# Giving GpSimd every fourth chunk of the weighting in the attention's second pass

## The chip, the cores and the metric

The kernel runs on one core of a Trainium2 chip. The metric is the device time of one execution in microseconds (us), median of several runs. The engines are named as in the profile: PE (TensorE), DVE (VectorE), ACT (ScalarE), POOL (GpSimd) and SP (SyncE, which only issues DMAs here).

## The reference

Four graph layers follow one another, each added to the node features and layer-normed. The change is in the third, graph attention: 3125 nodes of 256 features (8 heads of 32), 100000 edges sorted by destination.

```python
h = (x @ W.T).reshape(n, H, D)
h_src = h[src]
...
alpha = jnp.where(alpha >= 0, alpha, 0.2 * alpha)
amax = jax.ops.segment_max(alpha, dst, num_segments=n)
ex = jnp.exp(alpha - amax[dst])
denom = jax.ops.segment_sum(ex, dst, num_segments=n)
attn = ex / jnp.maximum(denom[dst], 1e-10)
out = jax.ops.segment_sum(h_src * attn[..., None], dst, num_segments=n)
return out.reshape(n, H * D) + bias
```

## The kernel before

The edges are padded and cut into `NCD` = 808 chunks of 128 edges, so that one chunk belongs to one block of 128 destination nodes; there are `NB` = 25 blocks. The attention has two passes over the chunks. The first (`logits_*`) gathers the source rows, writes them to `rows_spill` in HBM and keeps logits and running maxima in SBUF. The second (`sums_*`, with `carry_vector` ahead of it) makes the weighted sums. Since `denom` is the same for all edges of a node, it sums the unnormalised messages and the weights together, `TW` = 264 columns, and divides at the end (`attention_end_vector`).

For chunk c of the second pass:

- SP loads the 128 x 256 spilled rows into `hs`, a ring of `RB` = 16 slots in the tile `big`; slot c may be refilled when the rows of chunk c - 16 are weighted (L1972).
- ACT makes the one-hot matrices of four chunks at a time (`oh3`, L1996 and L1998), and the exponentials of four chunks at a time (L2005), written into columns 256 to 263 of the message buffers `msg`, a ring of 8 in the tile `ring`. The exponentials of group i (chunks 4i to 4i+3) wait until PE has summed chunk 4i - 5, since the buffers of group i - 2 must be free.
- `weighted_rows` (L1979) multiplies the 256 row entries by the weight of their head and writes `msg[:, c % 8, 0:256]`. It waits for the exponentials of its group, for the rows, and for PE having summed chunk c - 8. Both inputs, `hs` and the broadcast weights in `msg`, lie in SBUF.
- PE multiplies the one-hot matrix by the message into PSUM bank c % 8 (L2032, two MATMUL records for each chunk), in the order of the chunks.
- DVE adds the bank to the block's slice of the accumulator `hsrc`, in the tile `big` (L2069). The slice is picked by a number from a register; L83 loads sixteen such numbers at a time, L84 moves one. Two chunks in turn mostly add to the same slice, and so each add waits for the end of the add before:

```python
v.wait_ge(summed.s, summed.n(c + 1))
if c >= 1:
    v.wait_ge(added.s, added.n(c))
here = big[:, bass.ds(blk.at(c) * TW, TW)]
```

DVE's order is written out by hand in `sums_vector`: the weighting of chunk n, then the add of chunk n - 4, and so on. POOL has two instructions at the start of the pass, the cast L1984 of `off_last` into `away_b` and the memset L1985 of the accumulator, and then waits at the barrier `meet()` until the pass is over. Every engine's waits are on semaphores; `n(k)` is the count that k events give.

Of the kernel before, what the change touches and what calls it, by code (L numbers as in the profile page):

```python
# [9 lines left out]
def up(n, m):  # L10
    return -(-n // m) * m
# [17 lines left out]
NCD = up((E + (P - 1) * NB) // P, 8)  # L29
# [57 lines left out]
def program(nc, t, out):  # L87
    with ExitStack() as ctx:
        v, a, pe, g, sp = nc.vector, nc.scalar, nc.tensor, nc.gpsimd, nc.sync
        known = {}  # L90

        def signal(name):
            if name not in known:
                known[name] = Signal(ctx.enter_context(nc.semaphore(name)))
            return known[name]

        def again(old, count):

            new = Signal(old.s)
            new.over(old.base + count)  # L100
            return new
# [52 lines left out]
        def lanes(col, n, k):  # L154
            return col.rearrange("p (n o) -> p n o", o=1).to_broadcast([col.shape[0], n, k])
# [1589 lines left out]
        RB = 16  # L1745
# [219 lines left out]
        aways_made = again(mids_g, 0)  # L1965
        exps, msgs_v = again(step_done, NBATCH + 1), again(prefix_kept, NBATCH)

        def sums_sync():
            for c in range(NCD):
                if c >= RB:  # L1970
                    sp.wait_ge(msgs_v.s, msgs_v.n(c - RB + 1))
                sp.dma_start(hs[:, c % RB, :], rows_spill[c]).then_inc(spill.s(c, RB), 16)  # L1972

        def weighted_rows(eng, c):
            eng.wait_ge(exps.s, exps.n(c // 4 + 1))
            eng.wait_ge(spill.s(c, RB), spill.n(c, RB))
            if c >= 8:
                eng.wait_ge(summed.s, summed.n(c - 7))
            return eng.tensor_tensor(msg[:, c % 8, 0:D].rearrange("p (h d) -> p h d", h=H),  # L1979
                                     hs[:, c % RB, :].rearrange("p (h d) -> p h d", h=H),  # L1980
                                     lanes(msg[:, c % 8, D:TW], H, HD), ALU.mult)

        def sums_pool():
            g.tensor_copy(away_b[:, 1, :], off_last).then_inc(aways_made.s, 1)  # L1984
            g.memset(hsrc, 0.0).then_inc(accs_zeroed.s, 1)  # L1985

        def sums_scalar():
            a.copy(ident_b3, ident)
            a.copy(away_b[:, 0, :], off_first).then_inc(aways_made.s, 1)
            for n in range(NCD + 6):  # L1990
                if n < NCD and n % 4 == 0:
                    i, hot = n // 4, oh3[n // 4 % OH3]
                    if i >= OH3:
                        a.wait_ge(summed.s, summed.n(4 * (i - OH3) + 4))
                    for k in range(4):
                        ins = a.activation(hot[:, k, :], iota, ACT.Abs, bias=recd3[:, n + k, D_DL:D_DL + 1], scale=-1.0)  # L1996
                    then_a(ins)
                    a.activation(hot, hot, ACT.Relu, bias=1.0, scale=-1.0).then_inc(hot_made.s, 1)  # L1998
                c = n - 6
                if c >= 0 and c % 4 == 3:  # L2000
                    i = c // 4
                    a.wait_ge(lowered.s, lowered.n(1 if 4 * i + 4 <= CH else 2))
                    if i >= 2:
                        a.wait_ge(summed.s, summed.n(4 * i - 4))
                    a.activation(msg[:, 4 * (i % 2):4 * (i % 2) + 4, D:TW], alpha[:, 4 * i:4 * i + 4, :],  # L2005
                                 ACT.Exp).then_inc(exps.s, 1)

        def away_tensor(k):

            cs = slice(k // (2 * H) * CH, (k // (2 * H) + 1) * CH)  # L2010
            pe.matmul(ps[k % 8][:, 0:CH], ident_b3, away_b[:, k % 2, cs], start=True, stop=False)

        def sums_tensor():
            pe.wait_ge(aways_made.s, aways_made.n(2))
            for k in range(8):
                away_tensor(k)
            pe.wait_ge(carried.s, carried.n(1))
            for k in range(4 * H):
                half, h, reach = k // (2 * H), k // 2 % H, (fwd, bwd)[k % 2]
                if k >= 8:  # L2020
                    pe.wait_ge(carry_used.s, carry_used.n(k - 7))
                    away_tensor(k)
                pe.matmul(ps[k % 8][:, 0:CH], lanes(ident[0:H, h:h + 1], 1, P)[:, 0, :],
                          reach[:, half * CH:(half + 1) * CH], start=False, stop=True).then_inc(carry_spread.s, 1)
            pe.wait_ge(carry_used.s, carry_used.n(4 * H))
            pe.wait_ge(accs_zeroed.s, accs_zeroed.n(1))
            for c in range(NCD):
                pe.wait_ge(hot_made.s, hot_made.n(c // 4 + 1))
                pe.wait_ge(msgs_v.s, msgs_v.n(c + 1))
                if c >= 8:  # L2030
                    pe.wait_ge(added.s, added.n(c - 7))
                pe.matmul(ps[c % 8][:, 0:TW], oh3[c // 4 % OH3][:, c % 4, :], msg[:, c % 8, :],  # L2032
                          start=True, stop=True).then_inc(summed.s, 1)
# [22 lines left out]
        def sums_vector():  # L2056
            blk = Numbers(v, regs_v, blk_d_row, NB - 1)
            v.wait_ge(accs_zeroed.s, accs_zeroed.n(1))
            for n in range(NCD + 4):
                c = n  # L2060
                if c < NCD:
                    weighted_rows(v, c).then_inc(msgs_v.s, 1)
                c = n - 4
                if c >= 0:
# [4 lines that stand above are left out]
                    v.tensor_tensor(here, here, ps[c % 8][:, 0:TW], ALU.add).then_inc(added.s, 1)  # L2069
            v.wait_ge(added.s, added.n(NCD))  # L2070

        sums_sync()
        sums_pool()
        sums_scalar()
        sums_tensor()
        carry_vector()
        sums_vector()
        summed.over(NCD)
        added.over(NCD)
# [137 lines left out]
```

## Time and profile before

| | |
|---|---|
| median of 3 runs | 8846.99 us (8846.64 to 8849.97) |
| profiled execution, its own time | 8844.68 us |
| its span, first to last instruction | 8842.9 us |
| second pass's loop over the chunks, from the first weighting (L1979) | from 7024.5 us on; last L1979 starts at 7630.6 us |
| instructions of L1979, L2069 | 808 each, all on DVE |

The profile is of one execution. Busy time is the time in which an engine worked on instructions; an instruction's record covers its whole duration, and on DVE the next one can start before the record of the last has ended, so the distance from start to start says what an instruction costs a busy engine. Idle time is put down to what ended last before the engine went on.

### The profile page before, as it was taken

The page shows a single profiled execution, that of the slowest core. Times are in us where ns is not written, and L with a number is a line of the kernel's source. Part 1 is how long each engine was busy: PE and PEld are TensorE (multiplying, and loading weights), DVE is VectorE, ACT ScalarE, POOL GpSimd, SP SyncE. Part 2 cuts the span into 40 slices and gives each one's busy share as a digit, 9 for nine tenths or more (in the row PEclk, how much of TensorE's full clock was granted, in tenths as well). Part 3 has the DMA queues.
Part 4 walks back from the last instruction along what each step waited for, and adds up shares of the span by engine and source line. Part 5 has one row for each costly group of instructions (what it writes and reads, how often), then busy time and mean ns, then how long its engine had stood idle before and what let it go on. Part 6 is the DMA issues. An engine that isn't in the chain of part 4 may idle for free. (4 is left out here: it accounts for less than half of the span.)

```text
span 8842.9 us, 98679 instructions
## 1 busy us (share of the span) xinstructions
PE 5516.0 (62%) x21277; PEld 3079.4 (35%) x21277; DVE 5795.6 (66%) x15735; ACT 2945.2 (33%) x9436; POOL 5601.3 (63%) x5671
## 2 busy tenths in 40 slices
PE   2224980000677777777767777756767789687775
PEld 1113770000444444444532222343333333333332
DVE  8999980000777775555559999877777799833333
ACT  0000220000566652222238888733333366300000
POOL 5777777776777766777537777527777300077775
PEclk9999775555788888888869999977666699866665
DMA  2001320001555554555548888628888555333334
GB/s 94 6 6 40 117 86 11 3 3 38 158 166 159 160 143 148 166 161 166 151 120 242 242 242 242 175 80 243 244 243 243 136 175 176 102 105 105 105 105 87
DMA packets 796177, 1192.24 MB, mean 135 GB/s; under 512 B 161213, under 2 KB 631923, under 8 KB 788941
## 3 DMA queue, kind: packets, MB, share of 16 engines
q0 software_dynamic: 259712, 606.96, 26.1%
q1 hardware_dynamic: 535885, 578.95, 20.5%
q8 instruction: 192, 3.15, 0.1%
q14 instruction: 388, 3.18, 0.1%
HBM read 926.73 MB, written 258.64 MB: 134 GB/s over the span
## 5 line engine op out<-in xcount | busy, mean ns | idle before, releaser
L1178 POOL DMA_INDIRECT ring<-scaled_table,idx_s x832 | 787.3, 946 | 1024.9 <-DVEq L193 771.8
L1405 POOL DMA_INDIRECT big<-y_table,idx_s x832 | 859.5, 1033 | 480.3 <-issue 246.3
L1794 POOL DMA_INDIRECT ring<-att_table,rec_d_sb x808 | 778.9, 964 | 458.6 <-DVEq L193 206.4
L1473 PE MATMUL bank<-big,wts 128*128 128x512 f32 x1664 | 831.9, 623 | 364.0 <-DVE big L1397 364.0
L334 POOL DMA_INDIRECT rec_s<-acc,big x784 | 836.4, 1067 | 322.4 <-issue 256.5
L1034 POOL DMA_INDIRECT big<-x_table,rec_d_sb x808 | 812.2, 1005 | 300.5 <-issue 227.3
L2147 PE MATMUL bank<-ring,acc 128*128 128x256 f32 x1664 | 829.8, 621 | 239.3 <-DMA ring<-scaled_table,idx_s 202.3
L1178 POOL DMA_INDIRECT ring<-h_table,rec_d_sb x808 | 765.0, 947 | 310.7 <-issue 201.7
L334 POOL DMA_INDIRECT rec_d<-x_res,big x784 | 750.6, 957 | 255.7 <-issue 255.7
L1813 PE MATMUL bank<-big 128*128 x2424 | 594.4, 373 | 273.0 <-DVE acc L1904 219.0
L1215 PE MATMUL bank<-ring,acc 128*128 128x256 f32 x1616 | 549.0, 466 | 225.4 <-DMA ring<-h_table,rec_d_sb 222.6
L1421 ACT ACTIVATE big<-big,ring 128x64 f32<-128x64 f32 x2496 | 673.6, 332 | 19.3 <-DMA big<-y_table,idx_s 19.3
L1200 DVE TENSOR_TENSOR acc<-acc,bank 128x256 f32 x808 | 340.4, 421 | 461.2 <-PE bank L1215 239.9
L2137 DVE TENSOR_TENSOR acc<-acc,bank 128x256 f32 x416 | 175.3, 421 | 705.2 <-PEq L2150 630.4
L2147 PEld LDWEIGHTS bank<-ring,acc 128*128 128x128 f32 x1664 | 380.4, 277 | 688.5 <-DMA ring<-scaled_table,idx_s 637.6
L1473 PEld LDWEIGHTS bank<-big,wts 128*128 128x128 f32 x1664 | 284.8, 191 | 910.5 <-DVE big L1397 657.1
L2032 PE MATMUL bank<-ring 128*128 128x264 f32 x1616 | 545.8, 424 | 65.9 <-issue 58.8
L1139 PE MATMUL bank<-big,acc 128*128 128x256 f32 x1616 | 500.1, 454 | 116.4 <-DVE acc L1094 101.5
L1040 DVE MEMSET acc<- 128x512 f32 x1 | 0.5, 485 | 851.7 <-POOLq L193 851.7
L974 PE MATMUL bank<-ident,rec_d_sb 128*128 128x128 f32 x28 | 5.2, 373 | 868.8 <-DMA rec_d_sb<-rec_d 868.8
L1855 ACT ACTIVATE wts<-bank 128x256 f32<-128x256 f32 x808 | 310.2, 384 | 672.8 <-PE bank L1818 616.8
L833 ACT ACTIVATE big<-bank,big 128x128 f32<-128x128 f32 x832 | 312.6, 376 | 476.9 <-PE bank L801 474.5
(348 smaller groups left out, 12643.2 us busy)
## 6 DMA issues: line engine op xcount, KB each, us to landing
weights_dram<-big SPq DMA_DIRECT2D x104, 1024.0 KB
big<-weights_dram SPq DMA_DIRECT2D x832, 128.0 KB, 3.5
rows_spill<-ring SPq DMA_DIRECT2D x808, 128.0 KB
big<-rows_spill SPq DMA_DIRECT2D x808, 128.0 KB, 2.2
ring<-key_dram SPq DMA_DIRECT2D x49, 1024.0 KB
big<-dl_dram SPq DMA_DIRECT2D x50, 512.0 KB
big<-y_table,idx_s POOLq DMA_INDIRECT x832, 4.0
ring<-scaled_table,idx_s POOLq DMA_INDIRECT x832, 2.8
```

The lines of the kernel that those rows point to most:

```text
L334: g.indirect_dma_start(out=table, out_offset=bass.IndirectOffsetOnAxis(ap=row_of[k][:, j:j + 1], axis=0), in_=stage[:, j, :], in_offset=No ...
L1034: g.indirect_dma_start(out=xg[:, c % RG, :], out_offset=None, in_=x_table, in_offset=bass.IndirectOffsetOnAxis(ap=recd3i[:, c, D_IDX:D_IDX ...
L1139: ins = pe.matmul(quarter_bank(c), onehot[:, c % 16, :], xg[:, c % RG, 0:D], start=True, stop=True)
L1178: g.indirect_dma_start(out=slot[:, c % ring_len, :], out_offset=None, in_=table, in_offset=bass.IndirectOffsetOnAxis(ap=index(c), axis=0)) ...
L1215: ins = pe.matmul(quarter_bank(c), hot20[:, c % 20, :], hg[:, c % R2, :], start=True, stop=True)
L1405: g.indirect_dma_start(out=yg[:, n % RY, :], out_offset=None, in_=y_table, in_offset=bass.IndirectOffsetOnAxis(ap=idx_s[:, n:n + 1], axis= ...
L1421: ins = a.mul(dots[:, c % (2 * RM), d * MUL:(d + 1) * MUL], vectors[:, d * MUL:(d + 1) * MUL], sh3[:, c, d:d + 1])
L1473: pe.matmul(ps[4 + u % 4], oh1[c // 4 % 2][:, c % 4, :], mid[:, c % (2 * RM), 0:512], start=(c % 2 == 0), stop=(c % 2 == 1)).then_inc(summ ...
L1794: g.indirect_dma_start(out=ag[:, n % R3, :], out_offset=None, in_=att_table, in_offset=bass.IndirectOffsetOnAxis(ap=recd3i[:, n, D_IDX:D_I ...
L1813: ins = pe.matmul(ps[c % 3][:, 0:TW], hot_n[:, i % 3, k * P:(k + 1) * P], big_b[:, bass.ds(at + s * TW, TW)], start=(s == 0), stop=(s == 2))
L2032: pe.matmul(ps[c % 8][:, 0:TW], oh3[c // 4 % OH3][:, c % 4, :], msg[:, c % 8, :], start=True, stop=True).then_inc(summed.s, 1)
L2147: pe.matmul(ps[u % 8][:, 0:D], oh20[:, c % 20, :], sg[:, c % R4, :], start=(c % 2 == 0), stop=(c % 2 == 1))
```

## The change

In `weighted_rows` nothing changes. Chunks 3, 7, 11, ... are now weighted on POOL, which counts them on a new semaphore `msgs_by_pool`; DVE leaves them out and counts its own 606 on the old one. Whoever waits for a weighted chunk (PE before its matmul, SP before it refills a slot of `hs`) asks `rows_done`, which picks the semaphore by the chunk's number. The order of the adds on DVE, ACT's work and all buffers stay.

```diff
+        msgs_g = signal("msgs_by_pool")
+
+        def rows_done(eng, c):
+            if c % 4 == 3:
+                eng.wait_ge(msgs_g.s, msgs_g.n(c // 4 + 1))
+            else:
+                eng.wait_ge(msgs_v.s, msgs_v.n(c + 1 - (c + 1) // 4))
+
         def sums_sync():
             for c in range(NCD):
                 if c >= RB:
-                    sp.wait_ge(msgs_v.s, msgs_v.n(c - RB + 1))
+                    rows_done(sp, c - RB)
...
             g.memset(hsrc, 0.0).then_inc(accs_zeroed.s, 1)
+            for c in range(3, NCD, 4):
+                weighted_rows(g, c).then_inc(msgs_g.s, 1)
...
-                pe.wait_ge(msgs_v.s, msgs_v.n(c + 1))
+                rows_done(pe, c)
...
-                if c < NCD:
+                if c < NCD and c % 4 != 3:
                     weighted_rows(v, c).then_inc(msgs_v.s, 1)
```

The first place is DVE's queue in the middle of the pass, before. L1979 is a weighting, L84 the register move, L2069 an add:

```order
L84 ISA
L2069 TENSOR_TENSOR big<-big,bank 128x264
L1979 TENSOR_TENSOR ring<-big,ring 128x256
L84 ISA
L2069 TENSOR_TENSOR big<-big,bank 128x264
L1979 TENSOR_TENSOR ring<-big,ring 128x256
L84 ISA
L2069 TENSOR_TENSOR big<-big,bank 128x264
L1979 TENSOR_TENSOR ring<-big,ring 128x256
```

The same place now, where the weighting has line L1987 and the add L2079:

```order
L2079 TENSOR_TENSOR big<-big,bank 128x264
L1987 TENSOR_TENSOR ring<-big,ring 128x256
L84 ISA
L2079 TENSOR_TENSOR big<-big,bank 128x264
L84 ISA
L2079 TENSOR_TENSOR big<-big,bank 128x264
L1987 TENSOR_TENSOR ring<-big,ring 128x256
L84 ISA
L2079 TENSOR_TENSOR big<-big,bank 128x264
```

Once in four chunks two adds now stand next to each other, with no weighting between them.

The second place is POOL's queue, now, from the end of the first pass (L1794 is its gather) into the second; `blocks_counted` is the semaphore that counts the exponentials:

```order
L1794 DMA ring<-att_table,rec_d_sb 128x264 [waits mids_v,spill3]
L1992 CAST big<-rec_d_sb 128x808 [waits engines_met]
L1993 MEMSET big 128x6600
L1987 TENSOR_TENSOR ring<-big,ring 128x256 [waits spill3,blocks_counted]
L1987 TENSOR_TENSOR ring<-big,ring 128x256 [waits spill7,blocks_counted]
L1987 TENSOR_TENSOR ring<-big,ring 128x256 [waits summed,spill11,blocks_counted]
```

The three weightings shown are the first of 202; before, the memset was followed by the gathers of the fourth layer.

The third is PE's queue, now, in the middle of the pass (`prefix_kept` is the old count of weighted chunks):

```order
L2042 MATMUL bank<-ring 128x264 [waits added,msgs_by_pool,hot_made]
L2042 MATMUL bank<-ring 128x264 [waits added,prefix_kept,hot_made] x3
L2042 MATMUL bank<-ring 128x264 [waits added,msgs_by_pool,hot_made]
L2042 MATMUL bank<-ring 128x264 [waits added,prefix_kept,hot_made] x3
```

Before, all of them waited for `prefix_kept`; the order of the matmuls is the same.

## Rows read from the trace of the kernel before

**Rows 1.** The page: busy time of each engine.
```profile
span 8842.9 us, 98679 instructions
PE 5516.0 (62%) x21277; PEld 3079.4 (35%) x21277; DVE 5795.6 (66%) x15735; ACT 2945.2 (33%) x9436; POOL 5601.3 (63%) x5671
```

**Rows 2.** Engines by stretch: stretch, its length, busy (instructions), granted clock, DMA share, GB/s.
```profile
core 0: us, PE busy (x) PEld busy (x) DVE busy (x) ACT busy (x) POOL busy (x), PEclk, DMA share, GB/s
...
7024.50:7631.00 606.50, 544.99 (x1614) 241.50 (x1614) 550.49 (x1613) 400.32 (x1185) 0.00 (x0) 1.00 0.59 172
```

**Rows 3.** The instructions of L1979: count, shortest, median and longest duration.
```profile
L1979 DVE TENSOR_TENSOR ring<-big,ring x808: 408/418/426, 7024.5 to 7630.6; 128x256 f32<-128x256 f32 x162
```

**Rows 4.** Instructions in order of time, the middle of the pass: start, duration, engine, line.
```profile
7299.24 0.42 DVE L1979 TENSOR_TENSOR ring<-big,ring 128x256 f32<-128x256 f32 x1
...
7299.58 0.42 DVE L2069 TENSOR_TENSOR big<-big,bank 128x264 f32 x1
...
7299.92 0.42 DVE L1979 TENSOR_TENSOR ring<-big,ring 128x256 f32<-128x256 f32 x1
7300.25 0.42 DVE L2069 TENSOR_TENSOR big<-big,bank 128x264 f32 x1
7300.41 0.30 PEld L2032 LDWEIGHTS bank<-ring 128*128 128x128 f32 x2 [0.38 <-issue]
7300.54 0.23 ACT L2005 ACTIVATE ring<-acc 128x32 f32<-128x32 f32 x1 [0.64 <-PE bank L2032]
```

**Rows 5.** Instructions in order of time, DVE at the end of the pass.
```profile
7630.63 0.42 DVE L1979 TENSOR_TENSOR ring<-big,ring 128x256 f32<-128x256 f32 x1
7630.97 0.42 DVE L2069 TENSOR_TENSOR big<-big,bank 128x264 f32 x1
7631.61 0.43 DVE L2069 TENSOR_TENSOR big<-big,bank 128x264 f32 x1 [0.22 <-DVE big L2069]
7632.26 0.43 DVE L2069 TENSOR_TENSOR big<-big,bank 128x264 f32 x1 [0.22 <-DVE big L2069]
7632.91 0.43 DVE L2069 TENSOR_TENSOR big<-big,bank 128x264 f32 x1 [0.22 <-DVE big L2069]
```

**Rows 6.** The register loads L83 of the pass.
```profile
L83 DVEq TENSOR_LOAD <-unit_numbers x51: 1095/1099/1120, 7026.4 to 7627.7; - x51
```

**Rows 7.** Instructions in order of time, the pass's start, where PE had messages waiting.
```profile
7027.87 3.31 PE L2032 MATMUL bank<-ring 128*128 128x264 f32 x12
```

**Rows 8.** Instructions in order of time, POOL and DVE at the start of the second pass.
```profile
6950.56 1.83 DVE L2037 TENSOR_TENSOR_SCAN big<-rec_d_sb,norm 8x808 f32<-8x808 f32 x1 [1.29 <-ACTq L193]
6950.59 3.23 POOL L1984 CAST big<-rec_d_sb 128x808 bf16<-128x808 f32 x1 [16.43 <-ACTq L193]
...
6952.31 3.20 DVE L2038 TENSOR_TENSOR_SCAN big<-rec_d_sb,small 8x808 f32<-8x808 f32 x1
...
6953.77 5.59 POOL L1985 MEMSET big<- 128x6600 f32 x1
```

**Rows 9.** Groups by line and shape in the first pass: forward and reversed scans.
```profile
L1931 DVE TENSOR_TENSOR_SCAN ring<-ring 128x128 f32<-128x128 f32 x50 | 21.5, 429 | 4.5
L1926 DVE TENSOR_TENSOR_SCAN ring<-ring,bank 128x128 f32<-128x128 f32 x50 | 21.0, 420 | 3.7 <-issue 0.2
```

**Rows 10.** POOL's smallest memset, in the groups by line and shape.
```profile
L2207 POOL MEMSET const-float32-1.0<- 128x1 f32 x1 | 0.1, 104 | 0.0
```

**Rows 11.** The waits in the pass: who waited for whom, total, times, longest.
```profile
PE bank L2032 <- issue: 58.8, 60, 1.5
DVE big L2069 <- PE bank L2032: 55.3, 62, 1.4
PEld bank L2032 <- ACT ring L1998: 23.3, 59, 0.7
```

## The prediction

> **What bounds the kernel now.** I read the busy times first [rows 1]: no engine is near the whole span, so each stage has to be read by itself. The stage of the change is the loop over 808 chunks, and the view by stretches shows it [rows 2]: 606.5 us, with DVE busy for 550 us and PE for 545 us at a granted clock of 1.00 (the upper level, 2.4 GHz), POOL not at all, and the DMA engines 59% busy. Two engines near 90% can mean either, so I went to the order of time.
>
> There [rows 4] DVE alternates without a gap: a weighting at 7299.24, an add at 7299.58, a weighting at 7299.92, an add at 7300.25. From start to start it is 0.34 us each, 0.675 us for a chunk, and 807 x 0.675 = 545 us. The loop takes 606.1 us from the first to the last weighting [rows 3]; most of the other 61 us are the 51 register loads of 1.10 us each, 56 us [rows 6], which show as 62 adds that waited [rows 11]. PE is not the bound: each chunk's weights are loaded 0.07 us after its weighting ended (7299.92 + 0.42, against 7300.41 in [rows 4]), so PE takes each message as it comes; where messages were waiting for it, 12 matmul records, six chunks, took 3.31 us, 0.55 us a chunk [rows 7]. The pass runs at DVE's pace.
>
> Then the question is what DVE's 0.675 us consist of. The end of the pass answers it, where adds follow each other with no weighting between [rows 5]: they start at 7630.97, 7631.61, 7632.26 and 7632.91, 0.65 us apart, with 0.22 us idle each, released by the add before. An add waits for the end of the add before it (0.42 us), and semaphore, register move and start take the other 0.23 us. So the chain of adds alone needs 0.65 us a chunk, and the weighting lies almost wholly inside that wait.
>
> **The change, part by part.**
>
> *What is taken from DVE.* 202 weightings of 0.34 us of DVE's time, 68 us in a simple count. By the chain of adds, four chunks cost 3 x 0.675 + 0.65 = 2.675 us where they cost 2.70: the gain is 0.025 us in four chunks, 202 x 0.025 = 5 us. The 51 register loads stay as they are.
>
> *What POOL does.* 202 multiplications of two SBUF operands, 128 x 256, f32. No row has one, so I bound it. The memset of 6600 elements took 5.59 us [rows 8], 0.1 us of it fixed [rows 10], so a write costs 0.83 ns an element; at that rate 256 take 0.32 us, the lower bound. The cast of 808 elements is recorded with 3.23 us, but see below: it worked for 1.43 us, which is 1.65 ns an element beside the fixed part, so a read costs about 0.8 ns. Two reads and a write are then 2.45 ns, and 256 of them 0.63 us, 0.73 with the fixed part. I take 0.70 us. For the upper bound I take the cast's recorded 4.0 ns an element: 1.03 us. At 0.7 us in every 2.7 POOL has time enough, and PE gets POOL's chunk early: it may be made as soon as chunk c - 8 is summed, seven chunks ahead.
>
> The Trainium skill ("GPSIMD Engine Reference", section "Performance versus the Vector engine") gives 4497 ns for a two-input f32 operation of 2048 elements, about 2.6 cycles an element; as an estimate from that page 256 elements take 0.56 to 0.62 us. The sum below would by that be 12 to 21 us smaller. No row here shows it.
>
> *What it does to DVE.* The start of the pass has the one place where POOL and DVE both read SBUF in this kernel [rows 8]. DVE's scan L2037, with two SBUF inputs, starts at 6950.56 and takes 1.83 us; POOL's cast starts 0.03 us later and ends only at 6953.82. DVE's second scan L2038, of the same shape, starts at 6952.31 and takes 3.20 us, 1.37 more. That it runs backwards doesn't explain it: in the first pass forward and reversed scans take 420 and 429 ns [rows 9]. It fits one after the other: scan to 6952.39, cast to 6953.82 (1.43 us), second scan from there 1.69 us to 6955.51. So POOL's read and DVE's two-input instruction exclude each other for their whole length, on two instances. The memset that follows reads nothing.
>
> The Trainium skill ("SBUF — State Buffer", "Who interferes with whom") says the same as a rule: a DVE instruction with two SBUF inputs contends with a GpSimd instruction that reads SBUF, and the second to come blocks until the first is finished. It speaks against this change: the weightings have two SBUF inputs on both engines. The add has one of its two inputs in PSUM, and by that page doesn't contend; no row here shows an add beside a reading POOL.
>
> *Where in the period it hits.* Count from the start of DVE's weighting of chunk 4j+2 (0). The adds follow at 0.34 and 0.99, the weighting of 4j+4 at 1.33, an add at 1.66, weighting 4j+5 at 2.00, an add at 2.34, weighting 4j+6 at 2.675. POOL's next operation waits for exponentials that wait for PE having summed 4j+3. A weighting's start to the exponential that waits for its matmul is 1.30 us (7299.24 to 7300.54 in [rows 4]); the second matmul adds 0.55 [rows 7], the exponential 0.23, a semaphore 0.07: POOL may start at 2.15. DVE is then in weighting 4j+5 until 2.34. POOL runs from 2.34 to 3.04, under the add, and weighting 4j+6, due at 2.675, waits 0.36 us. Behind it in DVE's queue stands the add, so the whole chain of adds is late, and PE, which waits for that message, with it.
>
> In one period of four the register load (it stands behind the weighting of chunk 16k+4) holds DVE from about 1.66 to 2.77; POOL runs in that hole, from 2.15 to 2.85, and is done before the weighting behind it. That leaves 202 - 51 = 151 stalls: 151 x 0.36 = 54 us.
>
> *What else is added.* PE's and SP's waits only change their semaphore. POOL's queue has nothing behind the weightings but the barrier; the gathers of the fourth layer come after it. ACT waits in each group for PE now (0.64 us in [rows 4]) and keeps that slack. The rows' DMAs, 59% busy, are asked for a little more slowly. All this I cost at nothing. PE lies open wherever DVE stalls.
>
> *Sum.* -5 + 54 = +49 us. The profiled execution took 8844.68 us, 2.3 below the median of 8847; on the median the forecast is 8896 us, slower by 0.55%. By the bounds of POOL's operation: at 1.03 us the stall is 0.69, the sum +99 (8946 us); at 0.32 us it ends with the add and nothing stalls, -5 (8842 us).
>
> **The rivals.** A measurement of this kernel can tell about 0.2%, 18 us, from no change.
>
> *Contention as above* (forecast), 72% with POOL's operation between about 0.48 and 1.03 us. Another 7% I give to an operation longer than that, as with a slow broadcast operand: at 1.5 us each period loses about 1.1 us, the hole of the register load covers less, and it comes to over 200 us.
>
> *No exclusion between multiplications.* The scans may be special, and two instances are few. Then POOL's work is hidden, the chain of adds decides, and the time is 8842 us. 9%.
>
> *POOL asks later.* If POOL starts 0.5 us later than I reckon, after weighting 4j+6 has begun, it runs from 3.01 to 3.71, under the two adds that stand together; the next weighting is due at 4.0. No stall: 8842 us again. It decides at 2.675 against my 2.15. 8%.
>
> *DVE's instructions are the bound, not the chain* (the other side). If the second of the two adds needn't wait for the first, each period saves the whole 0.34 us: 68 us, less some stalls, 8779 to 8830 us. The 0.22 us of idle time at the end of the pass [rows 5] speaks against it; 4%.
>
> **How the numbers follow.** Slower by over 0.2% is 72 + 7, less 1 for stalls that come to under 18 us: 0.78. Within 0.2%: 9 + 8 and that 1: 0.18. Faster: 0.04. The range reaches from the cases without stalls, 8842, with a few us below, to the upper bound of POOL's operation, 8946, and a little over for the handing over at each conflict: 8838 to 8955 us. Outside lie the long operation and the faster case, about 11%, and a few per cent at the edges.
>
> **What would show it.** After the change the loop takes some 655 us from the first to the last weighting. POOL shows 202 multiplications, about 0.7 us by start and end, many starting while a weighting of DVE runs. DVE's 606 weightings are no longer all 0.42 us long: about a quarter of them (one in four chunks, save those at register loads) last about 0.36 us longer, or start that late. Some 200 adds have 0.22 us idle ahead of them, released by an add. If the weightings all keep 0.42 us and the loop is 600 us, the exclusion is wrong; if the adds stand closer than 0.65 us, the chain is wrong; if POOL's operation has another length, the stall changes by as much. The prediction fails most easily by POOL's length, and by where in the period POOL asks.

## The result and the profile after

The changed kernel takes 8875.1 us (median), the kernel before beside it 8848.9 us: a ratio of 1.0029, interval 1.0023 to 1.0035, 26 us slower. The profiled execution of after took 8879.5 us, its span is 8877.7 us, 34.8 more than that of before; of these two executions the parts are compared below. In the experiments' first two sets (e1 to e8) the kernel before took 10028 and 10040 us, in the third (e9 to e12) 8838 us; the added time lies in the stages with indirect DMAs, while the second pass's loop of an unchanged DVE queue takes 606 us in all of them (e1, e2, e8, e12), so e1 to e8 are read by this loop and by single instructions, and only e9 to e12 by totals too.

First the weightings of the pass and the adds, after (duration shortest, median, longest; first and last start):

```profile
L1987 DVE TENSOR_TENSOR ring<-big,ring x606: 411/420/833, 7052.7 to 7664.2; 128x256 f32<-128x256 f32 x152
L1987 POOL TENSOR_TENSOR ring<-big,ring x202: 614/840/844, 7019.7 to 7659.7; 128x256 f32<-128x256 f32 x101
```

```profile
  PE bank L2042: 54.6, 59
  DVE big L2079: 44.8, 203
  issue: 0.5, 2
```

The second fence is what the adds of L2079 waited for. Two things are to be seen. From DVE's first weighting to its last the loop takes 7664.2 - 7052.7 = 611.5 us, where it took 606.1 [rows 3]: 5.4 us more. And it begins 28 us later than before, 7052.7 against 7024.5. So in these two executions 28 of the 35 us were lost before the loop had begun, in stages whose code is the same.

The groups of the pass by line, where the mean of DVE's weighting has gone from 418 to 439 ns:

```profile
L2079 DVE TENSOR_TENSOR big<-big,bank 128x264 f32 x808 | 342.3, 424 | 99.9 <-PE bank L2042 54.6 <-DVE big L2079 44.8 <-issue 0.5
L1987 DVE TENSOR_TENSOR ring<-big,ring 128x256 f32<-128x256 f32 x606 | 265.9, 439 | 0.5
...
L1987 POOL TENSOR_TENSOR ring<-big,ring 128x256 f32<-128x256 f32 x202 | 156.3, 774 | 516.7 <-ACT ring L2015 516.7
```

One period of four chunks in order of time, the counterpart of [rows 4] (L2015 makes the exponentials, L2042 is the matmul):

```profile
7303.95 0.43 DVE L2079 TENSOR_TENSOR big<-big,bank 128x264 f32 x1 [0.22 <-DVE big L2079]
7304.29 0.42 DVE L1987 TENSOR_TENSOR ring<-big,ring 128x256 f32<-128x256 f32 x1
7304.63 0.42 DVE L2079 TENSOR_TENSOR big<-big,bank 128x264 f32 x1
7304.71 0.23 ACT L2015 ACTIVATE ring<-acc 128x32 f32<-128x32 f32 x1 [0.94 <-PE bank L2042]
...
7304.97 0.42 DVE L1987 TENSOR_TENSOR ring<-big,ring 128x256 f32<-128x256 f32 x1
7305.02 0.84 POOL L1987 TENSOR_TENSOR ring<-big,ring 128x256 f32<-128x256 f32 x1 [2.16 <-ACT ring L2015]
7305.30 0.42 DVE L2079 TENSOR_TENSOR big<-big,bank 128x264 f32 x1
...
7305.64 0.50 DVE L1987 TENSOR_TENSOR ring<-big,ring 128x256 f32<-128x256 f32 x1
```

POOL starts 0.05 us into a weighting of DVE and takes 0.84 us. The add between isn't touched. The next weighting, at 7305.64, takes 0.50 us in place of 0.42: it is held for 0.08 us.

Of the 606 weightings 137 are held, 131 of them for 0.08 us like this one. The other six are held for 0.13 to 0.41 us. In the longest case POOL had begun 0.06 us before DVE, and it kept its short duration:

```profile
7132.17 0.61 POOL L1987 TENSOR_TENSOR ring<-big,ring 128x256 f32<-128x256 f32 x1 [3.18 <-ACT ring L2015]
7132.23 0.83 DVE L1987 TENSOR_TENSOR ring<-big,ring 128x256 f32<-128x256 f32 x1
```

All 137 follow one rule to within 0.01 us: the weighting is held for what was left of POOL's record when it started, less 0.14 us (here 7132.78 - 7132.23 - 0.14 = 0.41). The seven weightings that started in the last 0.10 us of a record of POOL weren't held.

Ahead of the pass the difference is in POOL's indirect DMAs. The scatters L334 at the program's start, the gathers L1405 of a middle stage, the gathers L1794 of the first attention pass and L1178 of the last stage, before:

```profile
L334 POOL DMA_INDIRECT rec_s<-acc,big x784: 954/958/2535, 53.2 to 1161.2; - x196
L334 POOL DMA_INDIRECT rec_d<-x_res,big x784: 952/958/971, 1162.4 to 2167.5; - x196
...
L1405 POOL DMA_INDIRECT big<-y_table,idx_s x832: 942/949/1269, 4537.4 to 5695.4; - x167
...
L1794 POOL DMA_INDIRECT ring<-att_table,rec_d_sb x808: 942/946/2312, 5903.0 to 6933.2; - x162
...
L1178 POOL DMA_INDIRECT ring<-scaled_table,idx_s x832: 942/946/1032, 7731.1 to 8770.6; - x167
```

and after:

```profile
L334 POOL DMA_INDIRECT rec_s<-acc,big x784: 962/967/2599, 53.2 to 1164.7; - x196
L334 POOL DMA_INDIRECT rec_d<-x_res,big x784: 962/967/979, 1166.0 to 2177.5; - x196
...
L1405 POOL DMA_INDIRECT big<-y_table,idx_s x832: 947/957/1342, 4558.0 to 5716.4; - x167
...
L1794 POOL DMA_INDIRECT ring<-att_table,rec_d_sb x808: 948/953/2301, 5923.0 to 6960.1; - x162
...
L1178 POOL DMA_INDIRECT ring<-scaled_table,idx_s x832: 942/946/1062, 7765.0 to 8804.9; - x167
```

By the medians a scatter takes 9 ns more and a gather ahead of the second pass 7 or 8 ns more, from the program's first one on; behind the pass, in L1178, they are at 946 ns, as before the change. The scatters end 10.0 us later (2177.5 against 2167.5), and the first pass's gathers alone last 6.9 us longer (5923.0 to 6960.1 against 5903.0 to 6933.2). Not every stage passes it on: L1405 lasts 1158.4 us in place of 1158.0, though each of its 832 gathers is 8 ns longer.

### The profile page after: what moved, and what is told of

It is laid out like the page before. It is cut to its first block and busy times, and to the rows that moved or that the text cites. A ratio compares the mean times of both kernels' runs of the same rounds, so it can differ in the third digit from the quotient of the medians.

```text
span 8877.7 us, 98679 instructions
## 1 busy us (share of the span) xinstructions
PE 5492.4 (62%) x21277; PEld 3103.4 (35%) x21277; DVE 5762.4 (65%) x15533; ACT 2942.3 (33%) x9436; POOL 5790.4 (65%) x5873
## 5 line engine op out<-in xcount | busy, mean ns | idle before, releaser
L1405 POOL DMA_INDIRECT big<-y_table,idx_s x832 | 862.2, 1036 | 477.9 <-issue 244.8
L1794 POOL DMA_INDIRECT ring<-att_table,rec_d_sb x808 | 786.5, 973 | 457.0 <-DVEq L193 205.4
L334 POOL DMA_INDIRECT rec_s<-acc,big x784 | 841.7, 1074 | 320.7 <-issue 255.0
L1178 POOL DMA_INDIRECT ring<-scaled_table,idx_s x832 | 787.7, 947 | 357.6 <-issue 226.3
L1178 POOL DMA_INDIRECT ring<-h_table,rec_d_sb x808 | 770.8, 954 | 311.9 <-issue 196.3
L334 POOL DMA_INDIRECT rec_d<-x_res,big x784 | 757.8, 967 | 254.9 <-issue 254.9
L2042 PE MATMUL bank<-ring 128*128 128x264 f32 x1616 | 503.6, 417 | 113.9 <-issue 98.4
L1987 POOL TENSOR_TENSOR ring<-big,ring 128x256 f32<-128x256 f32 x202 | 156.3, 774 | 516.7 <-ACT ring L2015 516.7
```

What stands on the lines that cost most here:

```text
L334: g.indirect_dma_start(out=table, out_offset=bass.IndirectOffsetOnAxis(ap=row_of[k][:, j:j + 1], axis=0), in_=stage[:, j, :], in_offset=No ...
L1178: g.indirect_dma_start(out=slot[:, c % ring_len, :], out_offset=None, in_=table, in_offset=bass.IndirectOffsetOnAxis(ap=index(c), axis=0)) ...
L1405: g.indirect_dma_start(out=yg[:, n % RY, :], out_offset=None, in_=y_table, in_offset=bass.IndirectOffsetOnAxis(ap=idx_s[:, n:n + 1], axis= ...
L1794: g.indirect_dma_start(out=ag[:, n % R3, :], out_offset=None, in_=att_table, in_offset=bass.IndirectOffsetOnAxis(ap=recd3i[:, n, D_IDX:D_I ...
```

## The experiments

Two things were asked: what the pass owes to the chain of adds and to the contention, and where the 28 us ahead of it come from.

**e1: two counts, all weightings on DVE.**

```diff
-            for c in range(3, NCD, 4):
-                weighted_rows(g, c).then_inc(msgs_g.s, 1)
...
-                if c < NCD and c % 4 != 3:
-                    weighted_rows(v, c).then_inc(msgs_v.s, 1)
+                if c < NCD:
+                    weighted_rows(v, c).then_inc((msgs_g if c % 4 == 3 else msgs_v).s, 1)
```

> DVE weights all 808 chunks again, but counts every fourth on the new semaphore, as in the change; POOL does nothing in the pass. Theory (the 28 us ahead of the pass come with the multiplications in POOL's queue): POOL's gathers take 946 ns as before, the pass starts near 6951 us, its loop takes 606 us, the time is that of before within 3 us. Rival (the new semaphore or the moved waits cost it): gathers at 953 ns, the pass starts near 6979 us, about 28 us slower than before.

```profile
L1987 DVE TENSOR_TENSOR ring<-big,ring x808: 416/419/427, 8070.1 to 8676.3; 128x256 f32<-128x256 f32 x162
...
L1794 POOL DMA_INDIRECT ring<-att_table,rec_d_sb x808: 940/946/2312, 6645.3 to 7979.7; - x162
```

Ratio 1.0001 (0.9992 to 1.0011), loop 606.2 us, gathers 946 ns. The new semaphore and the waits on it cost nothing, in the pass or in the length of the gathers ahead of it.

**e2 and e8: one multiplication.** The kernel before, with a single multiplication of a constant 128 x 128 tile behind POOL's memset; e8 is e2 once more.

```diff
             g.memset(hsrc, 0.0).then_inc(accs_zeroed.s, 1)
+            g.tensor_tensor(ring[:, 5760:5760 + P], iota, iota, ALU.mult)
```

> The kernel before with one single POOL multiplication (128 x 128, of a constant tile into unused columns) behind the memset of the second pass. Theory (a POOL multiplication anywhere in the program slows the gathers that come before it): gathers at 953 ns up to the pass, start of the pass near 6979 us, loop 606 us, total +28 us. Rival (it takes the 202 of them, or is no matter of the multiplication): gathers at 946 ns, total within 3 us of before.

> The kernel before with a single multiplication on POOL, as e2_one_multiply, on whatever chip this call gets. Theory: gathers 7 to 12 ns longer ahead of the pass; on a chip whose DMAs keep up with POOL (span of before near 8850 us) the total is 25 to 45 us above before; on one where they don't (near 10000 us) it is that of before. Rival: gathers are longer but the total is that of before on both.

The gathers of e2 and, in the second fence, of e8:

```profile
L1794 POOL DMA_INDIRECT ring<-att_table,rec_d_sb x808: 951/957/2308, 6628.5 to 7959.2; - x162
```

```profile
L1794 POOL DMA_INDIRECT ring<-att_table,rec_d_sb x808: 947/953/2307, 6634.1 to 7965.3; - x162
```

957 and 953 ns against 946: one multiplication that runs at the pass's start makes the thousands of DMAs ahead of it slower, by 7 to 11 ns. The totals don't move here (0.9998, 0.9986 to 1.0010, and 0.9994, 0.9985 to 1.0004). In these sets the first pass took some 1330 us in place of 1030 for the same 808 gathers at nearly the same length, so POOL's own time was not what the stage waited for; whether one multiplication costs 28 us where it is, these two runs could not show. That it depends on the chip, as the expectation of e8 has it, isn't shown either: e8 and e9, which lie on the two sides, have the same chip number on record.

**e3: the fourth chunks left out.** DVE's queue is that of the change, nobody weights chunks 3, 7, ...; their columns stay zero.

```diff
             if c % 4 == 3:
-                eng.wait_ge(msgs_g.s, msgs_g.n(c // 4 + 1))
+                if eng is sp:
+                    sp.wait_ge(spill.s(c, RB), spill.n(c, RB))
...
+            g.memset(msg[:, 3, 0:D], 0.0)
+            g.memset(msg[:, 7, 0:D], 0.0)
             g.memset(hsrc, 0.0).then_inc(accs_zeroed.s, 1)
-            for c in range(3, NCD, 4):
-                weighted_rows(g, c).then_inc(msgs_g.s, 1)
```

> Leaves out part of the computation: every fourth chunk is weighted by nobody, its message columns are zero. DVE's queue is that of the change, POOL has no multiplication and PE doesn't wait for one. Theory (the chain of adds sets the pace): the loop takes 606 - 202 x 0.03 = 599 to 601 us, although 68 us of DVE's work are gone. Rival (DVE's instructions set it): about 540 us. For the part ahead of the pass: near 6951 us if the slow gathers come with POOL's multiplications.

The weightings, and the waits of the adds:

```profile
L1988 DVE TENSOR_TENSOR ring<-big,ring x606: 417/419/426, 8022.6 to 8621.6; 128x256 f32<-128x256 f32 x152
...
  PE bank L2043: 54.1, 57
  DVE big L2080: 45.2, 205
```

The loop takes 599.0 us. A quarter of the weightings, 68 us of DVE's instructions, is gone and the pass gains 7.1 us: 205 adds now wait 0.22 us each for the add before. Of DVE's own work and the chain of adds, the chain is shown as what keeps the rest.

**e4: POOL writes only.** After the same waits POOL writes zeros in place of its products, after a first memset of unused columns; like e3 it leaves out the products of the fourth chunks.

```diff
-                weighted_rows(g, c).then_inc(msgs_g.s, 1)
+                g.wait_ge(exps.s, exps.n(c // 4 + 1))
+                g.wait_ge(spill.s(c, RB), spill.n(c, RB))
+                if c >= 8:
+                    g.wait_ge(summed.s, summed.n(c - 7))
+                if c > 3:
+                    g.wait_ge(padded.s, c // 4)
+                g.memset(ring[:, 5760:6100], 0.0).then_inc(padded.s, 1)
+                g.memset(msg[:, c % 8, 0:D], 0.0).then_inc(msgs_g.s, 1)
```

> Leaves out part of the computation: in place of each of its 202 multiplications POOL, after the same waits, writes zeros (two memsets, 340 and 256 elements, about 0.7 us together), so that it reads nothing. Theory (DVE's weightings are held up by POOL's reads): no weighting of DVE longer than 0.43 us, loop 599 to 601 us. Rival (any work of POOL holds them, or the waits do): some 135 weightings at 0.50 us and a loop of 611 us as in the change. If the slow gathers come with the multiplication the pass starts near 6951 us, if with a longer POOL queue near 6979 us.

```profile
L1987 DVE TENSOR_TENSOR ring<-big,ring x606: 418/419/426, 8064.9 to 8664.0; 128x256 f32<-128x256 f32 x152
...
L1794 POOL DMA_INDIRECT ring<-att_table,rec_d_sb x808: 940/946/2313, 6642.8 to 7974.2; - x162
```

No weighting above 426 ns, loop 599.1 us, as with no POOL work at all. The two memsets (0.38 and 0.31 us) aren't a full match for the multiplication, though: nothing holds them, and so they are mostly over just before the next weighting starts (at 8312.32 against 8312.33 in one period). What the run shows is this. 146 first memsets began within 0.27 us of the start of a weighting, where in the change POOL's reads are kept off, and all took 381 or 382 ns. And 11 weightings began inside a memset; three of them had more than 0.14 us of it before them, and took 424 to 426 ns. So it is POOL's reading, not its writing, that shuts DVE out and is shut out; for DVE's side this rests on three cases. The gathers are at 946 ns although POOL's queue is longer by 404 instructions: the length of the queue isn't it, the multiplication is.

**e5: the third chunk of four.**

```diff
-            if c % 4 == 3:
+            if c % 4 == 2:
                 eng.wait_ge(msgs_g.s, msgs_g.n(c // 4 + 1))
             else:
-                eng.wait_ge(msgs_v.s, msgs_v.n(c + 1 - (c + 1) // 4))
+                eng.wait_ge(msgs_v.s, msgs_v.n(c + 1 - (c + 2) // 4))
...
-            for c in range(3, NCD, 4):
+            for c in range(2, NCD, 4):
...
-                if c < NCD and c % 4 != 3:
+                if c < NCD and c % 4 != 2:
```

> The change, but POOL weights chunks 2, 6, 10, ... (the third of each four) in place of the fourth. Theory (a weighting of DVE waits only where POOL's read of about 0.5 to 0.6 us meets it): counted from the weighting of chunk 4j, POOL asks at about 0.93 and reads until about 1.55, and DVE's two adjacent adds stand before the weighting at 2.0; no weighting is held, loop 599 to 601 us where the change had 611.5; POOL's gathers ahead of the pass at 953 ns or more. Rival (POOL's reads cost DVE the same wherever they lie): over 100 weightings above 0.45 us and a loop near 611 us.

The weightings of both engines, and two of them in order of time:

```profile
L1987 DVE TENSOR_TENSOR ring<-big,ring x606: 410/418/509, 8067.7 to 8669.1; 128x256 f32<-128x256 f32 x152
L1987 POOL TENSOR_TENSOR ring<-big,ring x202: 614/633/817, 8034.7 to 8663.9; 128x256 f32<-128x256 f32 x101
```

```profile
8299.77 0.42 DVE L1987 TENSOR_TENSOR ring<-big,ring 128x256 f32<-128x256 f32 x1
...
8300.02 0.64 POOL L1987 TENSOR_TENSOR ring<-big,ring 128x256 f32<-128x256 f32 x1 [3.16 <-ACT ring L2015]
```

The loop takes 601.4 us, 10 less than with the fourth chunk, and DVE's median is back at 418 ns; two weightings are held. The gathers ahead of the pass take 953 ns, and the total is that of before (1.0000, 0.9990 to 1.0009). POOL's operation is now 633 ns long, and its shortest 614. This also reads the 840 ns of the change: it starts 0.05 us after a weighting there and is 0.23 us longer than 614 ns; here it starts 0.25 us after one and is 0.02 us longer. Both say that a weighting of DVE keeps POOL off until about 0.28 us after its start, not for the 0.42 us of its record; 143 operations of the change and 150 of e5 give 0.27 to 0.29 us.

**e6 and e7: the register move ahead of the waits**, on e5 and on the kernel before.

```diff
+                    here = big[:, bass.ds(blk.at(c) * TW, TW)]
                     v.wait_ge(summed.s, summed.n(c + 1))
                     if c >= 1:
                         v.wait_ge(added.s, added.n(c))
-                    here = big[:, bass.ds(blk.at(c) * TW, TW)]
```

> As e5_third_of_four, with the register move of an add put ahead of its waits, so that it no longer lies between the end of one add and the start of the next. Theory (the chain of adds is what keeps the time that the left out weightings free): two adjacent adds come 0.50 to 0.56 us apart in place of 0.64, the loop takes 20 to 30 us less than e5, 572 to 582 us. Rival: the distance of adjacent adds stays at 0.64 and the loop at 600 us.

> The kernel before with the register move of an add ahead of its waits, nothing else. Theory (with a weighting between any two adds, DVE's own instructions already fill 0.675 us a chunk): loop 603 to 607 us, no gain. Rival (the chain of adds alone sets the pace before, too): adds come 0.55 us apart and the loop falls to about 500 to 550 us.

```profile
L2079 DVEq FUSED_REGOPS  x808: 57/57/72, 8075.4 to 8659.3; - x162
...
  DVE big L2079: 42.8, 203
```

The first row is the register operation that now stands at the add's line, the second what the adds waited for. This is e6, and both expectations failed in part. Loop times are 582.9 us (e6) and 594.2 us (e7), ratios 0.9970 (0.9960 to 0.9980) and 0.9986 (0.9973 to 0.9998). But the chain of adds was hardly shortened: a register operation of 57 ns still stands behind the waits, now at the add's own line, and 203 adds still wait 0.21 us each; adjacent adds start 0.63 us apart, where e5 has 0.64. What became shorter is the time lost at each register load. In e7, at one of them:

```profile
8401.34 0.42 DVE L1979 TENSOR_TENSOR ring<-big,ring 128x256 f32<-128x256 f32 x1
8402.52 0.43 DVE L2069 TENSOR_TENSOR big<-big,bank 128x264 f32 x1 [0.76 <-PE bank L2032]
8402.87 0.42 DVE L1979 TENSOR_TENSOR ring<-big,ring 128x256 f32<-128x256 f32 x1
```

1.53 us from weighting to weighting, where the kernel before has 1.70 to 1.82 us at 48 of its 51 loads, most of them near 1.78: 51 x 0.25 = 13 us, the 12 that e7 gained. The load itself takes 1.10 us in both; it no longer stands behind the add's wait, and at most places starts 0.22 us ahead of a weighting in place of 0.19 us behind one. Of e6's 18 us against e5, 13 lie where a weighting stands between two adds, the loads among them, and 4 at the adjacent adds.

**e9 to e12: where the multiplication stands.** e9 is the change again. e10 adds one multiplication at the program's start to it, ahead of all indirect DMAs; e12 adds only that one to the kernel before; e11 is e6 with it.

```diff
             g.wait_ge(made.s, 4)
+            g.tensor_tensor(ring[:, 5990:6090], iota[:, 0:100], iota[:, 0:100], ALU.mult)
```

> The change itself once more, as the reference of this call. Theory: pass's loop 611 us, gathers of POOL ahead of the pass 7 ns longer. On a chip with before near 8850 us: about 26 us slower; on one with before near 10030 us: 0 to 10 us slower.

> The change, with one more POOL multiplication (100 columns of a constant tile into unused ones) at the program's start, ahead of all indirect DMAs. In e8 and in the change the gathers go back to 946 ns once POOL has multiplied. Theory (the gathers are slow only until the first multiplication has run): gathers at 946 ns from the start, the pass starts as in the kernel before (near 6951 us on a chip of that kind), loop 611 us, total 3 to 10 us above before in place of 26. Rival (gathers are slow as long as multiplications still stand ahead in the program): 953 ns up to the pass, as in the change.

> POOL weights the third chunk of each four, the register moves stand ahead of the add's waits, and the early multiplication is there. If the gathers are back at 946 ns, its total is below before by the loop's 606 - 583 = 23 us, on either kind of chip; if not, on a chip near 8850 us it is 5 us above before.

> The kernel before with only the early multiplication. Theory: gathers at 946 ns throughout, total that of before within 3 us. Rival (a program that holds a multiplication of POOL has slow gathers, executed or not): gathers at 953 ns in all stages, 30 us slower on a chip near 8850 us.

| | median, before 8837.6 us | ratio, interval | gathers L1794, median | pass's loop |
|---|---|---|---|---|
| e9 | 8869.3 | 1.0035 (1.0021 to 1.0049) | 953 ns | 610.7 us |
| e10 | 8868.7 | 1.0035 (1.0022 to 1.0049) | 953 ns | 610.3 us |
| e11 | 8837.1 | 1.0002 (0.9993 to 1.0011) | 953 ns | 584.2 us |
| e12 | 8838.7 | 1.0001 (0.9992 to 1.0010) | 946 ns | 606.2 us |

The gathers of e10 and, in the second fence, of e12:

```profile
L1795 POOL DMA_INDIRECT ring<-att_table,rec_d_sb x808: 949/953/2307, 5916.6 to 6948.1; - x162
```

```profile
L1795 POOL DMA_INDIRECT ring<-att_table,rec_d_sb x808: 942/946/2313, 5901.3 to 6932.5; - x162
```

The theory that the first multiplication sets the DMAs right fell: in e10 one has run at the start, and they stay at 953 ns up to the pass. The rival held: they are slow as long as a multiplication still stands ahead in the program, and one that stands in front of them, e12, does nothing. The early one has 100 columns where that of e2 has 128; that this makes no difference is not tested by itself. The change's loss ahead of the pass comes again in e9: its loop is 4.6 us longer than before's, its total 32 us. In the profiled executions of this set the loop begins at 7022.9 us in e12, as before (7024.5), and at 7042.2, 7041.5 and 7050.4 us in e9, e10 and e11: 19 to 28 us are lost ahead of it. e11 has the fastest form of the pass that was tried with POOL, 22 us less than before, and ends level: the DMAs ahead take it back.

## Why the prediction was right, and where it was not

The side and the range held: 8875 us, where 8896 was forecast and 8838 to 8955 allowed. That the total is this near is partly luck. The loop, forecast to take 49 us more, takes 5 to 6 more, and most of the loss comes from something that the prediction put at nothing; with the loop alone the kernel would have been slower by under 0.1%. By the prediction's own steps:

- **What bounds the pass.** Right. The loop runs at DVE's pace, and the chain of adds lies under it at 0.65 us: e3.
- **What is taken from DVE**, 5 us. Right, with 7 us measured (e3, e4). Adjacent adds wait 0.22 us, 203 times.
- **What POOL does**, 0.70 us. Mis-sized: 0.61 us alone (the shortest of 202, in the change and in e5), inside the bounds of 0.32 and 1.03. The estimate that the prediction worked out from the Trainium skill ("GPSIMD Engine Reference", section "Performance versus the Vector engine"), 0.56 to 0.62 us, has it too. The 840 ns of its record are 0.61 of work and 0.23 of waiting.
- **What it does to DVE.** The mechanism is right: POOL's reads and DVE's weightings exclude each other (137 held weightings and 143 held operations of POOL in the change, no such thing in e3 and e4), and the add with its PSUM input runs beside POOL unhindered (7305.30). So the trace agrees with what "SBUF — State Buffer" of the Trainium skill ("Who interferes with whom") says of both.
- **Where in the period it hits.** The weighting that was named is the one held, chunk 4j+6, in 134 of 202 periods (forecast 151). The size of the hold is the term that failed: 0.08 us in place of 0.36. POOL came in at 0.28 us after the start of weighting 4j+5 in place of at its end by my count, 0.34; it worked 0.61 in place of 0.70 us; and it was ready for the next weighting's reads before its own record ended. (2.00 + 0.28) + 0.61 = 2.89 is the end of its record, 7305.86 in the period shown, yet the weighting due at 2.675 ends only 0.08 late, 0.14 less than the 0.22 that were left. In all, 0.36 - 0.06 - 0.09 - 0.14 is about 0.08. A hold counted from record to record, as the prediction had it from two scans and a cast, is too long at both ends. The sum over the pass is 13 us of longer weightings (mean 439 against 418 ns, 606 of them) in place of 54. With the 7 us gained that makes the 5 to 6 us by which the loop grew.
- **What else is added**, "all this I cost at nothing". This step was wrong, and it holds most of the result: 28 of the 35 us of the profiled executions, and 19 of 24 when e9 is set against e12. POOL's 4824 indirect DMAs ahead of the pass became 7 to 9 ns longer. It comes with a POOL multiplication that stands behind them in the program (e2, e8; e10 keeps it), not with the semaphore (e1), not with the length of POOL's queue (e4), and not with a multiplication in front (e12). At 8 ns each they would be 39 us. Less arrived: L1405, for one, passed on 0.4 of its 6.7 us. That the longer DMAs are what delays the loop rests on the two going together, in the change and in e9 to e12; no run lengthened the DMAs alone on executions near 8840 us.
- **The rivals.** No exclusion: refuted by the held weightings of the change, which e3 and e4 don't have. POOL asks later: not so in the change, where it asked 0.1 us earlier than reckoned (0.05 against 0.15 after the start of weighting 4j+5); e5, where POOL's reads meet almost no weighting, shows what that is worth, 10 us. A much longer operation: not so, 0.61 us. A much longer operation: not so, 0.61 us. DVE's instructions as the bound: refuted by e3.

What stays open is why the indirect DMAs take longer ahead of a multiplication that hasn't run yet. That the program's POOL code is laid out or held otherwise is one guess; no run here shows it.

## What to carry to other kernels

Before giving away work of a busy engine, look for a place where the remaining instructions stand alone, as at a loop's end: the distance there says what the engine keeps when the work is gone. Two engines whose reads shut each other out should be placed against each other by phase; moving POOL's quarter by one chunk took 10 us from the loop here and cost nothing. And compare the stages that the change doesn't touch as well, in the profile of after: most of this loss lay there, and a total that agrees with the forecast doesn't show that its terms do.

## What was not expected of the hardware

- One 128 x 128 multiplication on POOL, behind thousands of indirect DMAs in its queue, lengthens each of them by 7 to 13 ns (946 to 953 and 957 ns for gathers, 958 to 967 and 971 ns for scatters); behind it they are at 946 to 949 ns.
- A DVE weighting with a record of 0.42 us holds POOL's read off until about 0.28 us after its start, and POOL, whose two-input operation of 256 f32 elements takes 0.61 us, holds a weighting until 0.14 us before its own record ends.
- Moving the register load ahead of a wait took 12 us from the kernel before's pass (e7), with no change in any compute instruction: the load's 1.10 us then begin some 0.4 us earlier against the weightings.
